# Attention in a graph kernel: inverse softmax denominators by exp(-ln) on ScalarE in place of selection, widening and turning through TensorE

## The reference

```python
q, k, v = x @ qW + qb, x @ kW + kb, x @ vW + vb       # 8 heads of 16
scores = sum(q[src] * k[dst], axis=-1) / sqrt(16) + edge_attr @ eW + eb
mx  = segment_max(scores, dst)
ex  = exp(scores - mx[dst])
den = maximum(segment_sum(ex, dst), 1e-08)
attn = ex / den[dst]
out = segment_sum(v[src] * attn, dst) @ oW + ob        # then layer norms and an FFN
```

## Time and profile before

| | us |
|---|---|
| median of 3 runs (6049.87 to 6078.45) | 6054.59 |
| the profiled execution | 6070.21 |
| its span, first to last instruction | 6068.3 |
| its mean granted PE clock | 0.865 |

### The profile page before, as it was taken

One profiled execution on the slowest core, in us unless ns is written; L12 is line 12 of the kernel. 1 busy time (PEld: TensorE's weight loads), 2 busy tenths in 40 slices (PEclk: granted clock), 3 DMA queues, 4 the chain that ended last, 5 costly groups with the idle time before them and its releaser, 6 DMA issues. The chain is left out here.

```text
span 6068.3 us, 76920 instructions
## 1 busy us (share of the span) xinstructions
PE 4367.1 (72%) x16790; PEld 2619.4 (43%) x16790; DVE 4101.2 (68%) x13622; ACT 2768.2 (46%) x6238; POOL 3623.7 (60%) x3234
## 2 busy tenths in 40 slices
PE   6688859999998565545666579977896669936643
PEld 3355544444444333334444344534443334436643
DVE  6566658999998544447776576557665889836633
ACT  0233326777776010136666345534443446536643
POOL 4665638888886788845555661046204757855455
PEclk8787769999999777778888899989998889968876
DMA  6222223333332343356665575457544667757621
GB/s 213 62 76 72 73 66 88 99 100 98 98 98 75 74 62 62 59 102 198 187 199 181 169 210 161 131 150 216 172 141 141 176 161 204 202 163 226 190 78 54
DMA packets 767746, 802.51 MB, mean 132 GB/s; under 512 B 139776, under 2 KB 527944, under 8 KB 767162
## 3 DMA queue, kind: packets, MB, share of 16 engines
q1 hardware_dynamic: 405498, 393.44, 22.9%
q0 software_dynamic: 117504, 209.42, 14.6%
q10 hardware_dynamic: 244288, 194.72, 9.6%
HBM read 445.32 MB, written 351.92 MB: 131 GB/s over the span
## 5 line engine op out<-in xcount | busy, mean ns | idle before, releaser
L462 PE MATMUL gate_bank<-gate_ht,gate_whh 128*128 128x512 f32 x1764 | 872.4, 618 | 28.6 <-DVE gate_n L532 15.8
L925 POOL DMA_INDIRECT xh<-mean_xh,mean_pos_all x392 | 378.4, 965 | 338.9 <-DVE mean_xh L1027 142.2
L462 PEld LDWEIGHTS gate_bank<-gate_ht,gate_whh 128*128 128x128 f32 x1764 | 341.8, 202 | 407.0 <-issue 384.7
L2080 PE MATMUL back_ps_sums<-back_same,back_rows 128*128 128x512 f32 x400 | 286.6, 883 | 291.5 <-DMA back_rows<-x_a,back_idx 291.5
L151 POOL DMA_INDIRECT ffn_rows<-att_sums,ffn_idx x392 | 409.6, 1045 | 114.8 <-issue 106.3
L289 POOL DMA_INDIRECT gate_rows<-h_a,by_pos x200 | 197.8, 989 | 429.0 <-POOLq L117 328.4
L1521 PE MATMUL ffn_ps_f<-ffn_hg,ffn_f 128*128 128x512 f32 x784 | 407.1, 616 | 47.6 <-ACT ffn_hg L1698 47.6
L458 PE MATMUL gate_bank<-by_rank,gate_win 128*128 128x512 f32 x882 | 436.0, 594 | 0.0
L1514 PE MATMUL ffn_ps_u<-ffn_xs_t,ffn_up_w 128*128 128x512 f32 x784 | 387.0, 596 | 1.1 <-issue 1.1
L2061 POOL DMA_INDIRECT back<-back_out,back_dest x200 | 324.1, 1620 | 67.8 <-issue 60.1
L583 ACT ACTIVATE gate_z<-gate_bank,gate_b_rz 128x512 f32<-128x512 f32 x294 | 201.5, 685 | 346.0 <-PE gate_bank L462 225.6
(11 more groups left out here) (273 smaller groups left out, 12080.1 us busy)
## 6 DMA issues: line engine op xcount, KB each, us to landing
mean_x<-x_a SPq DMA_DIRECT2D x196, 256.0 KB
back<-blank ACTq DMA_DIRECT2D x99, 264.0 KB, 4.5
mean_rows<-back SPq DMA_DIRECT2D x98, 264.0 KB
hp<-mean_xh SPq DMA_DIRECT2D x98, 264.0 KB
gate_x<-xh SPq DMA_DIRECT2D x98, 264.0 KB
gate_hot<-hot_rows SPq DMA_DIRECT2D x100, 256.0 KB
ffn_x<-in_x_in SPq DMA_DIRECT2D x98, 256.0 KB
ffn_xr<-in_x_in SPq DMA_DIRECT2D x98, 256.0 KB
```

Of the source, the lines that this page charges most:

```text
L462: last = nc.tensor.matmul(bank_[:, :], whh[:, c * D:(c + 1) * D], ht[:, t.slot4, :], start=not inputs, stop=True)
L925: nc.gpsimd.indirect_dma_start(out=g["xh"][:, :], out_offset=bass.IndirectOffsetOnAxis(ap=pos_all[:, t.n, j:j + 1], axis=0), in_=xh[:, t.n ...
L2080: last = nc.tensor.matmul(ps_sums[t.slot][:, :], rows[:, t.slot4, j, :], same[:, t.slot, j, :], start=j == 0, stop=j == J - 1)
```

## The change

The chain over PE is taken out. ACT computes the logarithm of the whole `den` tile (128 x 512, `log`) and then the exponential of minus that (`inv`), for tile `now-4`, at the place where it widened the inverses of `now-5`, ahead of `ex`. DVE clamps `inv` at 1e8 (the bound that the maximum with 1e-8 gave) and multiplies it with `num` in one instruction, for tile `now-5`. The constants `heads`, the buffers `den_max`, `den_inv`, `inv_wide` and the PSUM bank `ps_inv` go. A dividing of `den` is nowhere left; the same values come out up to rounding.

```diff
             def step(tile_at):  # PE
-                if t := tile_at(6):
-                    wait(pe, wide_done, t.n + 1)
-                    wait(pe, max_done, min(t.n + 2, ET) if isinstance(t.n, int) else t.n + 2)
-                    for j in range(J):
-                        last = nc.tensor.transpose(edge_columns(ps_inv[:, :])[:, j, :],
-                                                   inv_wide[:, t.slot, j, :, :].rearrange("p h d -> p (h d)"),
-                                                   g["ident"][:, :])
-                    last.then_inc(inv_turned, 1)
...
-                if t := tile_at(4):
-                    wait(pe, den_done, t.n + 1)
-                    wait(pe, att_done, t.n - 1)
-                    wait(pe, max_done, t.n)
-                    for j in range(J):
-                        last = nc.tensor.matmul(ps_inv[:, j * HEADS:(j + 1) * HEADS],
-                                                edge_columns(den[:, t.slot, :])[:, j, :], heads[:, :],
-                                                start=True, stop=True)
-                    last.then_inc(den_made, 1)
...
             def step(tile_at):            # DVE
-                if t := tile_at(5):
-
-                    wait(dve, den_made, t.n + 1)
-                    nc.vector.tensor_scalar(den_max[:, t.slot, :, :].rearrange("p j h -> p (j h)"),
-                                            ps_inv[:, 0:J * HEADS], 1e-8, None, ALU.max).then_inc(max_done, 1)
-                    wait(dve, max_done, t.n + 1)
-                    wait(dve, wide_done, t.n - 1)
-                    nc.vector.reciprocal(...).then_inc(inv_done, 1)
...
-                if t := tile_at(6):
-                    wait(dve, inv_turned, t.n + 1)
+                if t := tile_at(5):
+                    wait(dve, inv_done, t.n + 1)
+                    wait(dve, num_done, t.n + 1)
                     wait(dve, out_made, t.n - 1)
-                    nc.vector.tensor_tensor(att[:, t.slot, :], num[:, t.slot4, :], ps_inv[:, :],
-                                            ALU.mult).then_inc(att_done, 1)
+
+                    nc.vector.scalar_tensor_tensor(att[:, t.slot, :], inv[:, t.slot, :], 1e8, num[:, t.slot4, :],
+                                                   ALU.min, ALU.mult).then_inc(att_done, 1)
...
-                    wait(dve, den_made, t.n - 1)
+                    wait(dve, log_done, t.n - 1)
...
             def step(tile_at):            # ACT
-                if t := tile_at(5):
-                    wait(act, inv_done, t.n + 1)
-                    wait(act, inv_turned, t.n - 1)
-                    nc.scalar.activation(
-                        inv_wide[:, t.slot, :, :, :].rearrange("p j h d -> p (j h) d"),
-                        den_inv[:, t.slot, :, :].rearrange("p j h -> p (j h)").unsqueeze(2).broadcast_to(
-                            [P, J * HEADS, HEAD_DIM]), ACT.Copy).then_inc(wide_done, 1)
+                if t := tile_at(4):
+                    wait(act, den_done, t.n + 1)
+                    wait(act, inv_done, t.n - 1)
+                    nc.scalar.activation(log[:, t.slot, :], den[:, t.slot, :], ACT.Ln).then_inc(log_done, 1)
+                    wait(act, log_done, t.n + 1)
+                    wait(act, att_done, t.n - 1)
+                    nc.scalar.activation(inv[:, t.slot, :], log[:, t.slot, :], ACT.Exp, scale=-1.0).then_inc(inv_done, 1)
```

More of the change, by code:

```diff
@@ L1088, in attention_pass @@
         blocks = f.sb("blocks", [P, HEADS, HEAD_DIM])
-        heads = f.sb("heads", [P, HEADS])
         idx = f.sb("idx", [P, 4, J, 2], I32)
@@ L1102, in attention_pass @@
         num = f.sb("num", [P, 4, SUPER])
-        den_max = f.sb("den_max", [P, 2, J, HEADS])
-        den_inv = f.sb("den_inv", [P, 2, J, HEADS])
-        inv_wide = f.sb("inv_wide", [P, 2, J, HEADS, HEAD_DIM])
         out = f.sb("out", [P, 2, SUPER])
-        ps_send, ps_recv, ps_q, ps_k, ps_v, ps_s, ps_inv, ps_out = (
-            f.ps(n) for n in ("ps_send", "ps_recv", "ps_q", "ps_k", "ps_v", "ps_s", "ps_inv", "ps_out"))
+        log, inv = f.sb("log", [P, 2, SUPER]), f.sb("inv", [P, 2, SUPER])
+        log_done, inv_done = f.sem("log_done"), f.sem("inv_done")
+        ps_send, ps_recv, ps_q, ps_k, ps_v, ps_s, ps_out = (
+            f.ps(n) for n in ("ps_send", "ps_recv", "ps_q", "ps_k", "ps_v", "ps_s", "ps_out"))
         w_loaded, consts_set, eb_made, eb_done, ew_done = (
@@ L1115, in attention_pass @@
          carry_done, top_done, arg0_done, drop_done, arg_done, ex_done, pv_done, den_done, num_done,
-         den_made, max_done, inv_done, wide_done, inv_turned, att_done, out_made, out_done) = (
+         att_done, out_made, out_done) = (
             f.sem(n) for n in ("rows_turned", "send_done", "recv_done", "q_made", "k_made", "v_made", "q_done",
                                "v_done", "qk_done", "s_made", "s_done", "carry_done", "top_done", "arg0_done",
[L1119 to L1122, removed]
+                               "drop_done", "arg_done", "ex_done", "pv_done", "den_done", "num_done", "att_done",
+                               "out_made", "out_done"))
+        loads = 11
         block = ctx.enter_context(nc.Block())
@@ L1130, in _ @@
                                (eb_row[:, :], g["eb"].rearrange("(a n) -> a n", a=1)),
-                               (blocks[:, :, :], g["blocks_c"]), (heads[:, :], g["heads_c"])):
+                               (blocks[:, :, :], g["blocks_c"])):
                 sp.dma_start(dst_, src_, allow_slow_non_contiguous=True).then_inc(w_loaded, 16)
@@ L1244, in step @@
             def step(tile_at):
-                if t := tile_at(5):
-                    wait(dve, den_made, t.n + 1)
-                    nc.vector.tensor_scalar(den_max[:, t.slot, :, :].rearrange("p j h -> p (j h)"),
-                                            ps_inv[:, 0:J * HEADS], 1e-8, None, ALU.max).then_inc(max_done, 1)
-                    wait(dve, max_done, t.n + 1)
-                    wait(dve, wide_done, t.n - 1)
-                    nc.vector.reciprocal(den_inv[:, t.slot, :, :].rearrange("p j h -> p (j h)"),
-                                         den_max[:, t.slot, :, :].rearrange("p j h -> p (j h)")).then_inc(inv_done, 1)
                 if t := tile_at(3):
```

## The result

The changed kernel takes 6028.68 us (median of 7 runs, 6022.26 to 6032.06), the kernel before 6068.44 in the same comparison (7 runs, 6049.87 to 6079.64): ratio 0.9939, 95% interval 0.9927 to 0.9952. So it is 40 us faster; the forecast was 61 us.

The account below looks back on a forecast made before the run. The prediction took POOL's gathers, held up by PE's late scores, and then a PE-only tail as the bound. Terms of 16, 30 and 15 us summed to 61 off 6054.6: 5994 by the median (6009 profiled), range 5945 to 6095.

Parts of the forecast that it names:

- the sum of 61 us: Attention stage: 16 us from short breaks, 30 from long breaks and 15 from the tail; chance 0.47.
- (a): POOL's short breaks, 32 us, from PE steps at a lowered clock: half goes with PE's shorter step, 16 us.
- (c): Tail after the last gathers, PE alone: less selection and transpose work gives 15 us; period about 8.5 us between den scans.
- POOL's pitch: Gathers in the attention stage start every 1.25 us at best, 0.95 and 0.30 of issue; eight per tile need 10.0 us.
- (b): POOL's 14 long breaks: one PE release less ahead of the scores' release saves 2.14 us in each, 30 us.
- The bound: Attention stage: POOL's 400 gathers, standing still when PE is late with scores for the index list, then a PE-only tail.
- Table loads: Rival, ACT between v and ex: Ln and Exp alternate, 100 loads, 128 us; 6070 by the median; chance 0.28.
- More late releases: Rival, POOL's gathers: every run is 16 long and ends in a long break, 25 for 14; 38 us slower; chance 0.17.
- The full cut: Rival, PE in the attention stage: all 131 us of removed PE work come off, 5923 by the median; chance 0.04.

Follow-up runs that it names:

- the other pair: Second executions of both kernels, unchanged, under condition A: kernel before 6110.5 us in its one execution; changed kernel 6057.58 against 6101.49, ratio 0.9939.
- one_set_late: Changed kernel with one table load for both functions, logarithm and exponential moved to the end of ACT's step: 6042.82 us, 0.9911 of the kernel before, condition A.
- lead2_c: Kernel before, with POOL allowed two tiles ahead of the turned rows, not three: 5561.82 us, ratio 1.0005, condition B.
- one_set_c: Changed kernel with one table load for both functions, placed by hand ahead of ACT's loop: 5571.18 us, 1.0025 of the kernel before, condition B.
- pe_busy_c: Changed kernel with one table load, PE doing the removed matmuls and transposes on idle data: 5578.95 us, 1.0036 of the kernel before, condition B.

## Why the prediction was right and where it was wrong

Under condition A the direction was right, and 6029 us lies inside 5945 to 6095; under B the same change is 22 us slower. The step that failed is the sum of 61 us. It took 31 us for PE's shorter step in the short breaks (a) and the tail (c), it put the table loads at nothing, and it held POOL's pitch at 1.25 us, so that it had no term for longer gathers. The runs show these places as a loss: 7 and 3 us for (a) in the two pairs, 1 us lost and 4 gained for (c), and 20 and 16 us for longer gathers and small gaps. That the stage came out at 54.7 and 41.5 us all the same is luck: the long breaks (b) gave 82 and 57 us for 30, and the errors cancel.

- *The bound.* Right: the stage's length is when POOL gets its index lists, plus the tail. The 55 us show up one for one in the last gather's start (37 of 41.5 in the other pair).
- *(b) Long breaks, 30 us: mis-sized, 82 and 57 us measured.* I let all 14 breaks stand, each shorter by one release, with the scores late in each. ACT waited for late scores only 8 times in that stage. In fact 10 of 14 breaks are gone (5 of 10 in the other pair); the scores' release is rarely among the late ones now. "Where a stall goes, say what is late next": it is mostly the turned rows, which POOL can do without where I looked.
- *(a) Short breaks, 16 us: wrong in sign.* They are as many by my count, 22 for 23, and 7 us dearer; counted by idle time they are 21 for 13. It looks as if a long break that goes leaves a short one behind, but no run shows that.
- *(c) The tail, 15 us: 1 lost and 4 gained under A* (71.7 us from the last gather to the stage's end for 71.0, and 78.2 for 82.5), 6 gained under B and 9 there with one load. The period that I had named for it, 8.5 us, comes in only a part of the tail's steps (8.2 to 11.7), and in all of one_set_late's. So it is the loads, or the place ahead of ex, that took it under A; the rival had said the loads.
- *Table loads: the case that I held less likely happened.* Its count (100), its 1.28 us each and the wait of pv were as worked out. Its conclusion, 16 us slower than the kernel before by the median, was wrong under A, because it made each long break longer by the chain when most of these breaks went away. Under B the changed kernel is 22 us slower, but that this is near 16 is chance: the 16 are made of long breaks, of which B has none. The cause of the forecast's error about the loads is that the profile of before has no Ln; one table load in the stage did not tell how the sets are chosen.
- *The missing term.* I took POOL's pitch as fixed, 0.95 us and 0.30. It isn't: the 400 gathers grew by 14 and 12 us under A (1.016 to 1.051 us each, 1.025 to 1.054), by 31 under B. The rows held the sign of it: a gather of 1.86 us in the earlier trace rows is nearly twice the last one, 0.94, and I didn't ask why.
- *More late releases (0.17).* Did not happen; late waits fell to a third (to half in the other pair). Its premise, that each run of 16 ends in a late release, does not hold: runs go on to 24 and 32 under A and to 400 under B.
- *The full cut.* Ruled out under B, where PE's work is worth 8 us at most; not tested under A.

The sum against the measured stage under A: 82 for long breaks, less 7, less 20 for gathers and small gaps (14 of it the gathers), less 1 in the tail, is 54, for 54.7 seen; in the other pair 57 less 3, less 16, and 4 in the tail, is 42, for 41.5. What stays open is what makes condition A and holds PE's releases back there, and whether it was PE's work or its two releases per tile that let the scores through in time; the runs meant to tell fell under B.

## What to carry to other kernels

When the bound is an engine that issues indirect gathers, price a change by what it does to the gathers: when their index lists are released, and what DVE is doing with two SBUF inputs as they start. When a change brings a second activation function into a loop, look for table loads in the trace and load the common set once by hand; put operations that nobody needs soon behind the one that is waited for. And measure again, at other times and on other chips, if the gain hangs on waits that nothing in the program explains: here its sign turned with them.

## What the runs showed of the hardware that was not expected

- Two conditions, the same kernel: 5559 to 5563 and 6068 to 6101 us by the medians. The attention stage differs by some 150 us, 107 of them POOL's 14 long breaks; in the gated layers and means there are 391 to 423 us more. The late releases are there as well: ACT's waits of over 1 us behind a PE instruction that had ended over 1 us before sum to some 430 us there in the kernel before (about 100 of them), and to 5 in lead2_c.
- Under B, cutting PE's busy time from 490 to 406 us of 530 lowered its granted clock from 0.92 to 0.80, and doing the work again on idle data brought it back to 0.91; q's matmul went from 773 to 880 ns and back to 772 (lead2_c, one_set_c, pe_busy_c).
- A gather that starts under a DVE operation with two SBUF inputs, clear of its first 0.09 and last 0.25 us, ends 0.75 to 0.83 us after it, up to 1.96 us long in place of 0.95.
- A table load takes 1283 ns, and the next activation starts 0.01 to 0.03 us after it on average (0.6 and 1.3 us of idle time in 50), as in the earlier trace rows.
